# The exact half of each activation's two-part form comes from a second ReLU on ScalarE instead of a copy on VectorE

## The chip, the core and the metric

The kernel runs on one core of a Trainium2 chip. The metric is the device time of one execution, in microseconds (us). Four engines matter: TensorE (PE; its weight loads are shown apart, as PEld), VectorE (DVE), ScalarE (ACT) and the queue that issues transfers (SP). Each takes its own instructions in program order, and they meet only through semaphores.

## What is computed

The reference is the top of a recommendation model: the dot products between all pairs of 27 embeddings of a sample, and then five dense layers.

```python
bottom_mlp_output = bottom_output[:, 0, :]                     # (2048, 128)
interaction = jnp.einsum('bnd,bmd->bnm', bottom_output, bottom_output)
interaction_flat = interaction[:, _TRIL_R, _TRIL_C]            # 351 pairs
x = jnp.concatenate([bottom_mlp_output, interaction_flat, zero_pad], axis=1)
x = jax.nn.relu(x @ W0.T + b0)     # 1024
x = jax.nn.relu(x @ W1.T + b1)     # 1024
x = jax.nn.relu(x @ W2.T + b2)     # 512
x = jax.nn.relu(x @ W3.T + b3)     # 256
return x @ W4.T + b4               # 1
```

All of it is float32.

## The kernel before, in words

**Two parts for each number.** TensorE multiplies in the type `f32r`, which holds fewer bits than float32. So every operand is kept as a high part, the value rounded to `f32r`, and a low part, the value minus its high part. A product is three matmuls (`product`, L790 to L792): low weights times high activations, high times high, high times low. Three matmuls of 512 columns follow one another every 0.69 us.

**Chunks, tiles and steps.** The 2048 samples are worked in 4 chunks of 512. In a chunk, layer 0 makes 8 output tiles of 128 features by 512 samples (4 steps of one product each), layer 1 makes 8 tiles (8 steps each), and after layer 1's tile m the four products of layer 2 that use tile m-1 follow (4 steps). Layer 3 makes two tiles and layer 4 the answer. Tiles of layers 0 and 1 alternate between the two PSUM banks of `work`; layers 2 and 3 use the banks of `acc`. Of the next chunk, layer 0's tile 0 is put ahead of this chunk's layer 3, and tile 1 behind it. In the first chunk layer 0 is made in two halves of 256 samples: the left ones by functions of their own (`relu_left`, `split_left`), which the change leaves alone, and the right ones by `relu` and `split`.

**Pairs for the next chunk.** While a chunk's layers run, TensorE also makes the dot products (grams) of the next chunk's samples. At steps that `plan` lists, some three steps apart, it does a half: four matmuls into the two banks of `gps` (`gram_half`, L815). ScalarE copies each half out with four instructions (L416), and TensorE may begin the next half only when they are done (`pe.wait_ge(grams_out, n)`). VectorE prepares the inputs (L546, L548), adds the copied grams (L564), and, four times a chunk, transposes them (L605) and picks the pairs (L609); TensorE turns these (L828), ScalarE writes their high part (L440) and VectorE their low part (L627).

**What happens to a tile.** When a tile is done, ScalarE's `relu` (L442) adds the bias, applies ReLU and writes float32 into one of the two slots of `act_out` (L448). VectorE's `split` (L630) rounds that into the high part `h1h` or `h2h` (L636), and subtracts this from the value for the low part `h1l` or `h2l` (L638). Three things wait for this:
- TensorE begins the tile after next when the ReLU of the bank's last tile is done (`relu_done`);
- TensorE uses a tile as activations when its low part is there (`split_done`); layer 4 takes the high part as soon as `hi_done` says so;
- ScalarE writes a slot of `act_out` when the tile two before has been split (`split_done`).

**Orders.** All loops are unrolled in one common order (`interleave`), and every engine takes its own instructions out of that: where the order says half, then tile, ScalarE copies the half first and then applies the ReLU, whichever is ready first. In the first chunk the weights of layers 1 to 3 are also split, at the steps in `W1_AT`, `W2_AT` and `W3_AT`: ScalarE writes their high parts (L475, L464, L468), VectorE their low parts (L662, L667, L672).

Of the kernel before, what the change touches and what calls it, by code (L numbers as in the profile page):

```python
# [75 lines left out]
def rec_program(nc, x_t, x0_t, w0, w1, w2, w3, w4, biases, b4, out):  # L76
    f32, f32r = mybir.dt.float32, mybir.dt.float32r
    ALU = mybir.AluOpType
    ACT = mybir.ActivationFunctionType

    ctx = ExitStack()
    with ctx:
        def sb(name, shape, dt=f32):
            return ctx.enter_context(nc.sbuf_tensor(name, shape, dt))

        def sem(name):
            return ctx.enter_context(nc.semaphore(name))
# [17 lines left out]
        bias = sb("bias", [P, MT0 + MT1 + MT2 + MT3])  # L105
# [15 lines left out]
        h1h, h1l = sb("h1h", [P, MT0, CHUNK], f32r), sb("h1l", [P, MT0, CHUNK], f32r)  # L121
        h2h, h2l = sb("h2h", [P, 2, CHUNK], f32r), sb("h2l", [P, 2, CHUNK], f32r)
# [5 lines left out]
        H3 = MT0 - MT2  # L128

        work = ctx.enter_context(nc.psum_tensor("work", [P, 2, BANK], f32))  # L130
        acc = ctx.enter_context(nc.psum_tensor("acc", [P, 4, BANK], f32))
# [27 lines left out]
        hi_done, split_done = sem("hi_done"), sem("split_done")  # L159
        logits_done, ysum_done, y_done, out_done = sem("logits_done"), sem("ysum_done"), sem("y_done"), sem("out_done")  # L160

        def ge(eng, s, value):

            if not (isinstance(value, int) and value <= 0):
                eng.wait_ge(s, value)

        def at_first(c):

            return isinstance(c, int) and c == 0
# [27 lines left out]
        def nth(c, layer, m, more=True):  # L197

            if layer == 0 and m < EARLY:
                return m if at_first(c) else TILES * c + (m - EARLY if m == 0 else m)  # L200
            first = {0: 0, 1: MT0, 2: MT0 + MT1, 3: MT0 + MT1 + MT2 + (1 if more else 0)}
            return TILES * c + first[layer] + m

        def slot(layer, m, more=True):
            return nth(0, layer, m, more) % 2 if (layer, m) != (0, 1) else 1
# [41 lines left out]
        def columns(c):  # L247

            return RIGHT if at_first(c) else slice(0, CHUNK)
# [31 lines left out]
        def interleave(c, on_half, on_turn, on_tile, after_tile, on_step=lambda step: None):  # L281

            half_at, turn_at = plans[c]
            step = 0

            def passed(steps):
                nonlocal step
                for step in range(step, step + steps):
                    if step in half_at:
                        on_half(half_at[step])  # L290
                    if step in turn_at:
                        on_turn(turn_at[step])
                    on_step(step)
                step += 1

            for m in range(EARLY, MT0):
                passed(KT0)
                on_tile(0, m)
            for m in range(MT1):
                passed(KT1)  # L300
                on_tile(1, m)
                if m:
                    passed(MT2)
                after_tile(m)
            passed(MT2)
# [98 lines left out]
        def _(act):  # L404
            def grams_from_psum(g, h):

                n = HALVES * g + h
                act.wait_ge(gram_done, n + 1)
                if h % 2 == 0 and h >= 4:
                    act.wait_ge(half_sums, SLICES * (g - 1) + h // 2 - 1)  # L410
                at = h % 2 * HALF_GROUPS
                for q in range(GROUP):
                    rows = slice(q * QUAD, (q + 1) * QUAD)
                    src = gps[rows].rearrange("p b (g w) -> p (b g) w", w=2 * P)[:, :, 0:2 * GCOLS]
                    src = src.rearrange("p g (t c) -> p g t c", c=GCOLS)
                    last = act.activation(grams2[rows, h // 2 % 2, at:at + HALF_GROUPS, :, :],  # L416
                                          src[:, :, :, q * EVEN:q * EVEN + INPUTS], ACT.Copy)
                last.then_inc(grams_out, 1)
# [16 lines left out]
            def pairs_hi_part(g, s, first=False):  # L435

                act.wait_ge(pairs_t, SUBS * g + s + 1)
                dst = featH[0:PAIRS_TILE, 1:KT0, s * SUB:(s + 1) * SUB]
                src = pair_bank(first)[0:PAIRS_TILE, 0:PAIR_TILES * SUB].rearrange("p (t b) -> p t b", b=SUB)
                act.activation(dst, src, ACT.Copy).then_inc(pairs_hi, 1)  # L440

            def relu(c, layer, m, bank, more=True):  # L442

                n, row = nth(c, layer, m, more), [0, MT0, MT0 + MT1, MT0 + MT1 + MT2][layer] + m
                act.wait_ge(tile_done, n + 1)
                ge(act, split_done, n - 1)
                cols = columns(c) if layer == 0 else slice(0, CHUNK)
                act.activation(act_out[:, slot(layer, m, more), cols], bank[:, cols], ACT.Relu,  # L448
                               bias=bias[:, row:row + 1]).then_inc(relu_done, 1)

# [11 lines left out]
            def w2_hi_part(n):  # L462
                act.wait_ge(w2_in[n], 16)
                act.activation(w2_part(w2h, n), w2_part(w2raw, n), ACT.Copy).then_inc(w2_hi, 1)  # L464

            def w3_hi_part():
                act.wait_ge(w3_in, 16)
                act.activation(w3h[:, :], w3raw[:, :], ACT.Copy).then_inc(w3_hi, 1)  # L468

            def w1_hi_part(m):  # L470
                act.wait_ge(w_in[m % 2], kept(m))
                if m >= 2:
                    act.wait_ge(tile_done, nth(0, 1, m - 2) + 1)
                    act.wait_ge(w1_kept[m % 2], kept(m - 2))
                act.activation(w1s[:, m % 2, 0, :], stage[:, m % 2, :], ACT.Copy).then_inc(w1_hi, 1)  # L475
# [21 lines left out]
            def body(c, more):  # L497
                def on_half(h):
                    if more:
                        grams_from_psum(c + 1, h)  # L500

                def on_turn(s):
                    if more:
                        pairs_hi_part(c + 1, s)

                def on_tile(layer, m):
                    relu(c, layer, m, work[:, m % 2, :])

                def after_tile(m):
                    pass  # L510

                def on_step(step):
                    if c == 0 and step in W1_AT:
                        w1_hi_part(W1_AT[step])
                    if c == 0 and step in W2_AT:
                        w2_hi_part(W2_AT[step])
                    if c == 0 and step == W3_AT:
                        w3_hi_part()

                interleave(c, on_half, on_turn, on_tile, after_tile, on_step)  # L520
                for m in range(MT2):
                    relu(c, 2, m, acc[:, m, :])
                if more:
                    relu(c + 1, 0, 0, work[:, 0, :])
                for m in range(MT3):
                    relu(c, 3, m, acc[:, m, :], more)
                if more:
                    relu(c + 1, 0, 1, work[:, 1, :])

            for m in range(EARLY):  # L530
                relu(0, 0, m, work[:, m, :])
            for c in range(CHUNKS):
                body(c, c + 1 < CHUNKS)

# [2 lines left out]
        def _(dve):  # L537
# [92 lines left out]
            def split(c, layer, m, hi, lo, more=True):  # L630


                n, cols = nth(c, layer, m, more), columns(c) if layer == 0 else slice(0, CHUNK)
                full, hi, lo = act_out[:, slot(layer, m, more), cols], hi[:, cols], lo[:, cols]
                dve.wait_ge(relu_done, n + 1)
                dve.tensor_copy(hi, full).then_inc(hi_done, 1)  # L636
                dve.wait_ge(hi_done, n + 1)
                dve.tensor_tensor(lo, full, hi.bitcast(f32), ALU.subtract).then_inc(split_done, 1)  # L638

            def answers(c):  # L640
# [89 lines left out]
            def body(c, more):  # L730
# [8 lines left out]
                def on_tile(layer, m):  # L739
                    if layer == 0:  # L740
                        split(c, 0, m, h1h[:, m, :], h1l[:, m, :])
                        if c and m == EARLY + 1:
                            answers(c - 1)
                        if c == 0 and m == MT0 - 1:
                            w1_lo_part(1)
                    else:
                        split(c, 1, m, h2h[:, m % 2, :], h2l[:, m % 2, :])
# [14 lines left out]
                for m in range(MT2):  # L762
                    split(c, 2, m, h1h[:, H3 + m, :], h1l[:, H3 + m, :])
# [245 lines left out]
```

## Time and profile before

| what | value |
|---|---|
| time, three runs | 484.17, 484.64, 485.58 us; median 484.64 |
| profiled execution: its own time | 484.05 us |
| profiled execution: its span | 482.3 us |
| mean granted clock of TensorE | 0.996 |
| busy: PE / PEld / DVE / ACT | 470.3 / 399.2 / 282.8 / 242.6 us |

The span runs from the first instruction to the end of the last; 1.8 us of the execution's own time lie around it. A busy share is the part of the span in which the engine had at least one instruction under way. For TensorE the ends of matmuls are modelled and neighbours overlap, so its busy time doesn't tell how well it is used: the distance between starts does.

### The profile page before, as it was taken

The page shows a single profiled execution, that of the slowest core. Times are in us where ns is not written, and L with a number is a line of the kernel's source. Part 1 is how long each engine was busy: PE and PEld are TensorE (multiplying, and loading weights), DVE is VectorE, ACT ScalarE, POOL GpSimd, SP SyncE. Part 2 cuts the span into 40 slices and gives each one's busy share as a digit, 9 for nine tenths or more (in the row PEclk, how much of TensorE's full clock was granted, in tenths as well). Part 3 has the DMA queues.
Part 4 walks back from the last instruction along what each step waited for, and adds up shares of the span by engine and source line. Part 5 has one row for each costly group of instructions (what it writes and reads, how often), then busy time and mean ns, then how long its engine had stood idle before and what let it go on. Part 6 is the DMA issues. An engine that isn't in the chain of part 4 may idle for free.

```text
span 482.3 us, 6717 instructions
## 1 busy us (share of the span) xinstructions
PE 470.3 (98%) x2495; PEld 399.2 (83%) x2495; DVE 282.8 (59%) x508; ACT 242.6 (50%) x580; POOL 0.7 (0%) x6
## 2 busy tenths in 40 slices
PE   8989999999997999999999999999999999999997
PEld 8979987878775888888888888888888888888885
DVE  4599779687765877575616877766624633110124
ACT  4996577758673366565653266665553321110112
POOL 0000000000000000000000000000000000000000
PEclk9999999999998999999999999999999999999999
DMA  8979555765273231843345141653224000434200
GB/s 306 379 253 390 175 163 187 253 218 190 87 270 139 85 101 39 307 150 134 103 183 212 44 141 37 219 222 130 87 96 167 1 0 1 175 101 161 87 1 1
DMA packets 18992, 72.28 MB, mean 150 GB/s; under 512 B 2448, under 2 KB 4496, under 8 KB 14864
## 3 DMA queue, kind: packets, MB, share of 16 engines
q1 hardware_dynamic: 18960, 71.86, 42.3%
q8 instruction: 20, 0.33, 0.3%
q14 instruction: 12, 0.10, 0.1%
HBM read 63.45 MB, written 8.40 MB: 149 GB/s over the span
## 4 chain that ended last, share of the span: by engine, by line
PE 82%; DVE 9%; DMA 4%; ACT 2%; issue 2%; SPq 0%; DVEq 0%; ACTq 0%
PE work L790 18%; PE work L792 17%; PE work L791 17%; PE gps L815 8%; PE acc L790 7%; PE acc L791 6%; PE acc L792 6%; DMA xraw<-x_t 4%; DVE turned L605 2%; ACT grams L416 1%; PE acc L912 1%; DVE turned L594 1%; PE gps L828 1%; DVE w1s L662 1%; DVE pairs L609 1%
## 5 line engine op out<-in xcount | busy, mean ns | idle before, releaser
L416 ACT ACTIVATE grams<-gps 32x216 f32<-32x216 f32 x384 | 131.5, 343 | 86.0 <-PE gps L815 82.5
L790 PE MATMUL work<-h1h,w1s 128*128 128x512 f32 x256 | 101.7, 397 | 0.5 <-DVE w1s L662 0.4
L792 PE MATMUL work<-h1l,w1s 128*128 128x512 f32 x256 | 100.4, 392 | 0.0
L791 PE MATMUL work<-h1h,w1s 128*128 128x512 f32 x256 | 100.2, 391 | 0.0
L448 ACT ACTIVATE act_out<-work,bias 128x512 f32<-128x512 f32 (+1 forms) x64 | 42.3, 662 | 90.9 <-PE work L792 89.6
L815 PEld LDWEIGHTS gps<-xs 128*128 128x128 f32 x384 | 56.6, 190 | 10.0 <-issue 1.4
L636 DVE CAST h2h<-act_out 128x512 fp32r<-128x512 f32 x40 | 17.0, 426 | 76.5 <-ACT act_out L448 76.5
L815 PE MATMUL gps<-xs 128*128 128x224 f32 x384 | 58.3, 274 | 0.4 <-DVE featL L627 0.3
L790 PE MATMUL work<-featH,w0l 126*128 126x512 f32 (+5 forms) x160 | 56.7, 354 | 1.1 <-ACT act_out L448 0.6
L792 PEld LDWEIGHTS work<-h1l,w1s 128*128 128x128 f32 x256 | 48.1, 188 | 10.6
L790 PEld LDWEIGHTS work<-h1h,w1s 128*128 128x128 f32 x256 | 48.3, 189 | 9.3 <-DVE w1s L662 1.4
L792 PE MATMUL work<-featL,w0h 126*128 126x512 f32 (+5 forms) x160 | 55.7, 348 | 0.0
L791 PE MATMUL work<-featH,w0h 126*128 126x512 f32 (+5 forms) x160 | 55.7, 348 | 0.0
L564 DVE SCALAR_TENSOR_TENSOR grams<-grams 128x216 f32<-128x216 f32 x48 | 18.4, 383 | 63.1 <-ACT grams L416 62.9
L791 PEld LDWEIGHTS work<-h1h,w1s 128*128 128x128 f32 x256 | 48.4, 189 | 7.8
L790 PE MATMUL acc<-h2h,w2l 128*128 128x512 f32 x128 | 51.5, 402 | 3.0 <-DVE h2l L638 2.5
L548 DVE TENSOR_TENSOR xs<-xraw,xs 128x864 fp32r<-128x864 f32 x48 | 50.8, 1059 | 1.7
L791 PE MATMUL acc<-h2h,w2h 128*128 128x512 f32 x128 | 50.8, 397 | 0.0
L792 PE MATMUL acc<-h2l,w2h 128*128 128x512 f32 x128 | 50.8, 397 | 0.0
L636 DVE CAST h1h<-act_out 128x512 fp32r<-128x512 f32 (+1 forms) x48 | 19.3, 402 | 25.6 <-ACT act_out L448 25.4
L790 PEld LDWEIGHTS work<-featH,w0l 126*128 126x128 f32 (+2 forms) x160 | 30.1, 188 | 5.0 <-issue 1.0
L792 PEld LDWEIGHTS work<-featL,w0h 126*128 126x128 f32 (+2 forms) x160 | 30.0, 187 | 4.2
(71 smaller groups left out, 520.5 us busy)
## 6 DMA issues: line engine op xcount, KB each, us to landing
xraw<-x_t SPq DMA_DIRECT2D x64, 432.0 KB, 4.2
w1s<-w_parts SPq DMA_DIRECT2D x24, 1024.0 KB, 4.8
w_parts<-w1s SPq DMA_DIRECT2D x8, 1024.0 KB, 4.8
stage<-w_t SPq DMA_DIRECT2D x8, 512.0 KB, 5.9
w0raw<-w_t SPq DMA_DIRECT2D x4, 512.0 KB, 8.0
w2raw<-w_t SPq DMA_DIRECT2D x4, 512.0 KB, 9.0
x0raw<-x_t SPq DMA_DIRECT2D x4, 256.0 KB, 5.3
w3raw<-w_t SPq DMA_DIRECT2D x1, 512.0 KB, 10.5
```

The source lines that it names most:

```text
L416: last = act.activation(grams2[rows, h // 2 % 2, at:at + HALF_GROUPS, :, :], src[:, :, :, q * EVEN:q * EVEN + INPUTS], ACT.Copy)
L448: act.activation(act_out[:, slot(layer, m, more), cols], bank[:, cols], ACT.Relu, bias=bias[:, row:row + 1]).then_inc(relu_done, 1)
L548: dve.tensor_tensor(lo, by_sample(xraw, p), hi.bitcast(f32), ALU.subtract).then_inc(xl_done, 1)
L564: dve.scalar_tensor_tensor(out=grams[:, at:at + SLICE_GROUPS, :], in0=grams2[:, p % 2, :, 0, :], scalar=0.5, in1=grams2[:, p % 2, :, 1, :] ...
L594: dve.transpose(turned[:, :, :], first_grams(s).rearrange("p g m -> p m g")).then_inc(turned_done, 1)
L605: dve.transpose(turned[:, :, :], grams[:, :, :].rearrange("p g m -> p m g")).then_inc(turned_done, 1)
L609: dve.tensor_tensor(dst, one, other, ALU.add).then_inc(pairs_done, 1)
L636: dve.tensor_copy(hi, full).then_inc(hi_done, 1)
L790: pe.matmul(dst, wl, ah, start=start, stop=False)
L791: pe.matmul(dst, wh, ah, start=False, stop=False)
L792: return pe.matmul(dst, wh, al, start=False, stop=stop)
L815: last = pe.matmul(gps[:, j // 2, j % 2 * 2 * P:j % 2 * 2 * P + 2 * GCOLS], xs[:, p % XSLOTS, 0, four, :].rearrange("p b n -> p (b n)"), x ...
```

## The change

`relu` gets one more instruction, ahead of the old one: a ReLU of the same PSUM tile with the same bias, written as `f32r` directly to the high part. `split` loses its rounding copy and only subtracts. The semaphore `hi_done` is now raised by ScalarE. The waits ahead of `relu` now stand ahead of both its instructions. TensorE's and SP's programs stay as they are.

```diff
@@ scalar
-            def relu(c, layer, m, bank, more=True):
+            def relu(c, layer, m, bank, hi, more=True):
                 n, row = nth(c, layer, m, more), [0, MT0, MT0 + MT1, MT0 + MT1 + MT2][layer] + m
                 act.wait_ge(tile_done, n + 1)
                 ge(act, split_done, n - 1)
                 cols = columns(c) if layer == 0 else slice(0, CHUNK)
+                act.activation(hi[:, cols], bank[:, cols], ACT.Relu, bias=bias[:, row:row + 1]).then_inc(hi_done, 1)
                 act.activation(act_out[:, slot(layer, m, more), cols], bank[:, cols], ACT.Relu,
                                bias=bias[:, row:row + 1]).then_inc(relu_done, 1)
...
-                    relu(c, layer, m, work[:, m % 2, :])
+                    relu(c, layer, m, work[:, m % 2, :], h1h[:, m, :] if layer == 0 else h2h[:, m % 2, :])
...
-                    relu(c, 2, m, acc[:, m, :])
+                    relu(c, 2, m, acc[:, m, :], h1h[:, H3 + m, :])
...
@@ vector, in split
                 full, hi, lo = act_out[:, slot(layer, m, more), cols], hi[:, cols], lo[:, cols]
+                dve.wait_ge(hi_done, n + 1)
                 dve.wait_ge(relu_done, n + 1)
-                dve.tensor_copy(hi, full).then_inc(hi_done, 1)
-                dve.wait_ge(hi_done, n + 1)
                 dve.tensor_tensor(lo, full, hi.bitcast(f32), ALU.subtract).then_inc(split_done, 1)
```

The other calls of `relu` get their high part in the same way. The inserted line makes the old ReLU line L449 of the changed kernel, and its new one L448.

ScalarE, first chunk, layer 1, a place where the high part of a block of `w1` is written just ahead of a tile's ReLU. Before:

```order
L475 ACTIVATE w1s<-stage 128x1024
L448 ACTIVATE act_out<-work,bias 128x512
L416 ACTIVATE grams<-gps 32x216 x4
L464 ACTIVATE w2h<-w2raw 128x1024
L416 ACTIVATE grams<-gps 32x216 x12
```

Now:

```order
L476 ACTIVATE w1s<-stage 128x1024
L448 ACTIVATE h2h<-work,bias 128x512
L449 ACTIVATE act_out<-work,bias 128x512
L416 ACTIVATE grams<-gps 32x216 x4
L465 ACTIVATE w2h<-w2raw 128x1024
L416 ACTIVATE grams<-gps 32x216 x12
```

One instruction more stands between the block of weights and the copying of the next half.

VectorE at the end of the first chunk's layer 1: the last grams are added, transposed and picked, and then the last tile is split. Before:

```order
L564 SCALAR_TENSOR_TENSOR grams<-grams 128x216
L605 STREAM_TRANSPOSE turned<-grams 128x864
L609 TENSOR_TENSOR pairs<-turned 128x144
L609 TENSOR_TENSOR pairs<-turned 128x72
L609 TENSOR_TENSOR pairs<-turned 128x36
L609 TENSOR_TENSOR pairs<-turned 128x72
L609 TENSOR_TENSOR pairs<-turned 128x54
L636 CAST h2h<-act_out 128x512
L638 TENSOR_TENSOR h2l<-act_out,h2h 128x512
```

Now:

```order
L565 SCALAR_TENSOR_TENSOR grams<-grams 128x216
L606 STREAM_TRANSPOSE turned<-grams 128x864
L610 TENSOR_TENSOR pairs<-turned 128x144
L610 TENSOR_TENSOR pairs<-turned 128x72
L610 TENSOR_TENSOR pairs<-turned 128x36
L610 TENSOR_TENSOR pairs<-turned 128x72
L610 TENSOR_TENSOR pairs<-turned 128x54
L638 TENSOR_TENSOR h2l<-act_out,h2h 128x512
```

The rounding copy is gone; nothing else moved.

## Rows read from the trace of the kernel before

**Rows 1.** The page: busy us, share, count; share of the last chain.

```profile
PE 470.3 (98%) x2495; PEld 399.2 (83%) x2495; DVE 282.8 (59%) x508; ACT 242.6 (50%) x580; POOL 0.7 (0%) x6
...
PE 82%; DVE 9%; DMA 4%; ACT 2%; issue 2%; SPq 0%; DVEq 0%; ACTq 0%
```

**Rows 2.** Groups by form: count, busy us, mean ns, idle before.

```profile
L448 ACT ACTIVATE act_out<-work,bias 128x512 f32<-128x512 f32 x56 | 38.6, 689 | 88.9 <-PE work L792 87.7 <-DVE h1l L638 0.4
...
L638 DVE TENSOR_TENSOR h2l<-act_out,h2h 128x512 fp32r<-128x512 f32 x40 | 27.7, 692 | 1.4
...
L636 DVE CAST h2h<-act_out 128x512 fp32r<-128x512 f32 x40 | 17.0, 426 | 76.5 <-ACT act_out L448 76.5
```

**Rows 3.** Timeline, first chunk's layer 0: start us, us, instruction.

```profile
56.13 0.84 ACT L448 ACTIVATE act_out<-work,bias 128x256 f32<-128x256 f32 x2
...
56.66 0.39 PE L790 MATMUL work<-featH,w0l 128*128 128x256 f32 x1 [0.58 <-ACT act_out L448]
...
63.64 0.47 ACT L448 ACTIVATE act_out<-work,bias 128x256 f32<-128x256 f32 x1
...
64.24 0.45 PE L790 MATMUL work<-h1h,w1s 128*128 128x512 f32 x1
```

**Rows 4.** Timeline, first chunk's layer 1, weights ahead of a ReLU.

```profile
90.12 0.69 ACT L448 ACTIVATE act_out<-work,bias 128x512 f32<-128x512 f32 x1
...
90.71 1.39 ACT L416 ACTIVATE grams<-gps 32x216 f32<-32x216 f32 x4
...
92.20 0.68 PE L815 MATMUL gps<-xs 128*128 128x224 f32 x4
```

**Rows 5.** Timeline, the same pattern twice more.

```profile
102.55 0.68 PE L815 MATMUL gps<-xs 128*128 128x224 f32 x4
...
103.30 0.19 PEld L790 LDWEIGHTS work<-h1h,w1s 128*128 128x128 f32 x1 [0.25 <-DVE w1s L662]
...
133.66 1.39 ACT L416 ACTIVATE grams<-gps 32x216 f32<-32x216 f32 x4
...
135.17 0.66 PE L815 MATMUL gps<-xs 128*128 128x224 f32 x4
```

**Rows 6.** Timeline, a wait of TensorE for pairs.

```profile
81.01 0.42 DVE L636 CAST h2h<-act_out 128x512 fp32r<-128x512 f32 x1
...
83.69 0.55 DVE L627 TENSOR_TENSOR featL<-gps,featH 126x384 fp32r<-126x384 f32 x1
...
84.38 0.68 PE L815 MATMUL gps<-xs 128*128 128x224 f32 x4 [0.34 <-DVE featL L627]
```

**Rows 7.** Timeline, end of the first chunk's layer 1.

```profile
142.35 0.38 DVE L564 SCALAR_TENSOR_TENSOR grams<-grams 128x216 f32<-128x216 f32 x1 [2.45 <-ACT grams L416]
...
145.66 0.42 DVE L636 CAST h2h<-act_out 128x512 fp32r<-128x512 f32 x1
...
146.12 0.69 DVE L638 TENSOR_TENSOR h2l<-act_out,h2h 128x512 fp32r<-128x512 f32 x1
...
146.87 0.68 PE L790 MATMUL acc<-h2h,w2l 128*128 128x512 f32 x1 [2.54 <-DVE h2l L638]
```

**Rows 8.** Sums of a stretch: us, busy of PE, PEld, DVE, ACT, POOL, clock, DMA.

```profile
147.00:150.40 3.40, 3.40 (x9) 2.62 (x10) 0.00 (x0) 0.00 (x0) 0.00 (x0) 0.50 0.56 234
```

**Rows 9.** Timeline, second chunk's layer 0.

```profile
173.85 0.69 ACT L448 ACTIVATE act_out<-work,bias 128x512 f32<-128x512 f32 x1
...
174.96 1.40 ACT L416 ACTIVATE grams<-gps 32x216 f32<-32x216 f32 x4 [0.42 <-PE gps L815]
...
176.84 0.61 PE L815 MATMUL gps<-xs 128*128 128x224 f32 x4
```

**Rows 10.** Timeline, the last chunk's layers 2 and 3.

```profile
468.50 1.38 ACT L448 ACTIVATE act_out<-acc,bias 128x512 f32<-128x512 f32 x2 [2.74 <-PE acc L792]
...
472.87 0.69 DVE L638 TENSOR_TENSOR h1l<-act_out,h1h 128x512 fp32r<-128x512 f32 x1
...
473.62 0.50 PE L790 MATMUL acc<-h1h,w3l 128*128 128x512 f32 x1
```

More of the change, by code:

```diff
@@ L521, in body @@
                 for m in range(MT2):
-                    relu(c, 2, m, acc[:, m, :])
+                    relu(c, 2, m, acc[:, m, :], h1h[:, H3 + m, :])
                 if more:
-                    relu(c + 1, 0, 0, work[:, 0, :])
+                    relu(c + 1, 0, 0, work[:, 0, :], h1h[:, 0, :])
                 for m in range(MT3):
-                    relu(c, 3, m, acc[:, m, :], more)
+                    relu(c, 3, m, acc[:, m, :], h2h[:, m, :], more)
                 if more:
-                    relu(c + 1, 0, 1, work[:, 1, :])
+                    relu(c + 1, 0, 1, work[:, 1, :], h1h[:, 1, :])
             for m in range(EARLY):
-                relu(0, 0, m, work[:, m, :])
+                relu(0, 0, m, work[:, m, :], h1h[:, m, :])
             for c in range(CHUNKS):
```

## The prediction

> **What bounds the kernel now.** Start at the top of the page: TensorE is busy 98% of the span, VectorE 59% and ScalarE 50%, and 82% of the last chain is TensorE's [rows 1]. So work taken from VectorE or given to ScalarE counts only where TensorE waits for one of them. The second view is the list of TensorE's waits, read together with the timeline around each. Nearly all lie in the first chunk, where the other two engines also split the weights, and at the very end. Two kinds are to be seen. TensorE may wait for **ScalarE's queue**: for a ReLU that frees a `work` bank [rows 3], or for the copying of a half of the grams, which stands behind a ReLU [rows 4, 5]. And it may wait for **VectorE's queue**: for pairs [rows 6] or for the low part of a tile [rows 7, 10]. In chunks two and three TensorE doesn't wait: the copying ends at 174.96 + 1.40 = 176.36, and TensorE begins the next half at 176.84 [rows 9].
>
> **The prices.** A rounding copy costs VectorE 0.43 us, with the gap behind it 0.46 (145.66 to 146.12) [rows 2, 7]. A ReLU of 512 columns costs ScalarE 0.69 [rows 2]. The new ReLU has no row of its own, and the question is how much later it makes what comes behind it. The upper bound is its whole 0.69 (0.47 for 256 columns). The lower bound is what rows show of neighbours that overlap: two ReLUs of 256 columns take 0.84 together where one takes 0.47 [rows 3], so the second begins 0.10 early; and a copying begins at 90.71, 0.10 before the ReLU of 90.12 + 0.69 = 90.81 ends [rows 4]. The pair at the end that takes 1.38, twice 0.69 [rows 10], looks like the other bound, but there the second tile is finished just 0.69 behind the first (three matmuls), so its ReLU couldn't begin sooner. In the new order both ReLUs of a tile have the same waits, so nothing holds the second back. I take **0.59 for 512 columns and 0.37 for 256**.
>
> The Trainium skill ("ScalarE: Activation LUTs", section "What ACT_TABLE_LOAD costs") says the same of neighbours, "Back-to-back ACTIVATEs overlap by ≈ 93 ns", and the 0.10 above agrees. Its section "Rules for kernel authors" speaks against the change: for ReLU and the like "Use VectorE, not ScalarE". The durations here agree in direction, 0.43 on VectorE against 0.59 to 0.69 on ScalarE. By that rule alone all 88 tiles would be a loss; by the rows only those count for which TensorE waits, and the sum goes by these.
>
> **Part 1, added to ScalarE.**
> - *Start of layer 0, right half.* TensorE begins tile 4 at 56.66, 0.06 behind the first of the two ReLUs (56.13 + 0.47) [rows 3]. That ReLU is now second in its pair: **+0.37**. Layer 1's first tile begins at 64.24, 0.13 behind the ReLU of 63.64 + 0.47 [rows 3]: hardly any room, so again **+0.37**.
> - *Weights ahead of a ReLU.* Three times a block of weights and a ReLU stand between two copyings. The copying ends at 90.71 + 1.39 = 92.10 and TensorE's next half starts at 92.20, as soon as it may; the third place is the same, 133.66 + 1.39 = 135.05 against 135.17 [rows 4, 5]. Each pays the full 0.59. At the second, TensorE waits right afterwards for a block of `w1` from VectorE, until 103.30, and that wait isn't moved; 0.23 of its 0.25 us cover the delay [rows 5]. Sum: 3 x 0.59 - 0.23 = **+1.54**.
> - *Chunks two and three.* After a ReLU at 173.85 the next copying could begin at 173.85 + 2 x 0.59 = 175.03, instead of 174.96 [rows 9]: 0.07 late. Up to three such ReLUs follow each other, so 0.2 late; the copying has 0.48 - 0.10 = 0.38 to spare. **0**. With 0.69 a ReLU it would be 1.40 + 1.38 = 2.78 for a half that comes every 2.5 us (three steps of 0.69 and some 0.4 for the half itself), the spare time would be gone at the second ReLU, and each chunk would lose about 1.1.
>
> **Part 2, removed from VectorE.**
> - *Pairs.* TensorE waits 0.34 for `featL` at 84.38, which VectorE begins late, at 83.69, because it is busy without a break from before the copy of 81.01 [rows 6]. Without that copy most of the wait goes: **-0.3**.
> - *Low part of the last tile of layer 1.* TensorE waits 2.54 us, until 146.87. The chain is: grams added at 142.35, transposed, picked, copy at 145.66, subtraction at 146.12 [rows 7]. The ReLU was long done. Without the copy: **-0.46**. What is late next is the transposing, which nothing here touches.
> - The copies before 142 don't help here: VectorE had stood idle 2.45 us before 142.35, waiting for ScalarE [rows 7].
>
> **Part 3, the end.** The last chunk has no layer 0 to hide layer 3's start. Before, VectorE sets the pace with a copy and a subtraction a tile; the last subtraction begins at 472.87 and TensorE goes on at 473.62 [rows 10]. Now ScalarE sets it: eight ReLUs from 468.50 end at 468.50 + 7 x 0.59 + 0.69 = 473.32, plus 0.03, plus a subtraction of 0.69, plus 0.05 is 474.09: **+0.47**. The last tile of layer 3 then pays 0.59 - 0.46 = **+0.13**. In the other chunks layer 0's tile 0 (12 matmuls, 2.75 us) stands before layer 3 and covers this.
>
> Elsewhere a tile has 2 us or more until it is used (four products of layer 2, or most of a layer 1 tile), and the high parts that layer 4 takes come 0.4 sooner on ScalarE, but its low parts decide.
>
> **Sum.** 0.74 + 1.54 - 0.3 - 0.46 + 0.60 = **+2.1 us**: 484.05, the profiled execution's own time, becomes 486.2. The median shown is 0.59 above that execution, so I forecast **486.7** for the median. About 0.3%, 1.5 us, is what a measurement of this kernel can tell from no change.
>
> **The rivals.**
> - **A, the two ReLUs don't overlap** (0.69 each). The terms become 0.94, 3 x 0.69 - 0.2, -0.3, -0.46; chunks two and three lose 1.1 each; the first chunk's layer 3 waits 0.7, since ScalarE needs 8 x 0.69 = 5.5 us for four tiles and TensorE has 2.75 + 3 x 0.69 = 4.8 us of other work before it wants the fourth; the end takes 8 x 0.69 less what it takes now, 1.2, and 0.23. Sum 6.5: **491.2**. For it: a new destination type. Against: [rows 3, 4].
> - **B, TensorE's clock doesn't fall.** The granted clock was 0.50, 1.2 GHz, from 147.0 to 150.4, just after the wait of 2.54 us [rows 8, 7]. Half the speed over 3.4 us costs 1.7. The wait becomes 2.54 - 0.46 = 2.1 us, and if the clock stays up, the sum is 2.1 - 1.7 = +0.4, **485.0**, no change. The spread of the three runs, 1.4 us, is of this size, so this could come and go.
> - **C, VectorE's relief decides (the other side).** If VectorE's own backlog, and not ScalarE, were what makes the chain of 142.35 late, all delays of ScalarE in the first chunk would vanish in the 2.54 us wait, and seven copies of layer 1 less would end that wait: -2.5 + 0.6 = -1.9, **482.7**. It decides if VectorE no longer stands idle before L564. Against it are the 2.45 us of idle time there [rows 7].
> - **D, small delays add up elsewhere**, where the copyings have 0.38 to spare: 487.5 to 489.
>
> **How the numbers follow.** Forecast 0.50, of which 0.09 within 0.3% of before (its own range is 485.5 to 488.0); A 0.14; B 0.18, nearly all within; C 0.13; D 0.05. Slower 0.41 + 0.14 + 0.03 = 0.58, no change 0.09 + 0.18 = 0.27, faster 0.15, which takes C and the lower edge of B. The range 483.9 to 490.0 leaves out C and the upper half of A.
>
> **What the profile of the changed kernel would show.** L448 and L449 0.58 to 0.59 apart (A: 0.69). In the three places TensorE's half starts 0.6 later behind the block of weights. VectorE's last subtraction of the first chunk's layer 1 starts right behind the picking of pairs, and TensorE's wait there is 2.1 us. In chunks two and three the halves stay 2.5 us apart. The last chunk's layer 3 goes on 0.5 later. The forecast would be wrong if two of the three ScalarE places cost nothing, or if the clock behaves otherwise than before.

## The result, and the profile after

| | before | changed |
|---|---|---|
| median of 20 runs | 484.73 us | 486.37 us |
| lowest and highest | 482.92, 487.03 us | 485.03, 487.76 us |
| profiled execution: own time, span | 484.05, 482.3 us | 486.30, 484.5 us |

The changed kernel takes 1.0036 times the time of before (95% interval 1.0024 to 1.0049): 1.2 to 2.4 us slower. The medians are 1.64 us apart. The forecast was +2.1 us, to 486.7.

The page of the changed kernel, in answer to [rows 1]:

```profile
PE 470.5 (97%) x2495; PEld 399.0 (82%) x2495; DVE 248.5 (51%) x420; ACT 286.5 (59%) x668; POOL 0.7 (0%) x6
```

VectorE lost 34 us of work and ScalarE gained 44, each more than twenty times what the kernel lost. Since TensorE's program is the same, its instructions can be matched one by one. How far each begins behind its twin of before changes only in a few places; all differences in the account below were read that way.

**How two ReLUs stand to each other.** The changed kernel's timeline, ScalarE in the second chunk's layer 0, and TensorE's halves there, in answer to [rows 9]:

```profile
175.34 0.69 ACT L448 ACTIVATE h1h<-work,bias 128x512 fp32r<-128x512 f32 x1
175.93 0.68 ACT L449 ACTIVATE act_out<-work,bias 128x512 f32<-128x512 f32 x1
176.50 1.38 ACT L416 ACTIVATE grams<-gps 32x216 f32<-32x216 f32 x4
177.91 0.69 ACT L448 ACTIVATE h1h<-work,bias 128x512 fp32r<-128x512 f32 x1
178.50 0.68 ACT L449 ACTIVATE act_out<-work,bias 128x512 f32<-128x512 f32 x1
179.06 1.39 ACT L416 ACTIVATE grams<-gps 32x216 f32<-32x216 f32 x4
...
175.81 0.60 PE L815 MATMUL gps<-xs 128*128 128x224 f32 x4
178.34 0.61 PE L815 MATMUL gps<-xs 128*128 128x224 f32 x4
180.87 0.60 PE L815 MATMUL gps<-xs 128*128 128x224 f32 x4
```

A ReLU takes 0.69 but the next begins 0.57 to 0.60 behind its start (median 0.585 over 80 pairs), and the copying 0.57 behind the second one. ScalarE is now without a break here, yet TensorE's halves stay 2.53 us apart: the copying ends at 176.50 + 1.38 = 177.88, 0.46 ahead of 178.34.

**A place that pays.** The changed kernel's timeline where a block of `w1` stands ahead of the ReLUs, in answer to [rows 4]:

```profile
90.10 1.06 ACT L476 ACTIVATE w1s<-stage 128x1024 fp32r<-128x1024 f32 x1
91.19 0.69 ACT L448 ACTIVATE h2h<-work,bias 128x512 fp32r<-128x512 f32 x1
91.77 0.68 ACT L449 ACTIVATE act_out<-work,bias 128x512 f32<-128x512 f32 x1
92.34 1.38 ACT L416 ACTIVATE grams<-gps 32x216 f32<-32x216 f32 x4
...
93.82 0.34 PE L815 MATMUL gps<-xs 128*128 128x224 f32 x1 [0.60 <-issue]
```

The copying ends at 93.72 and TensorE begins at 93.82, as closely behind as before. TensorE now stands idle 0.60 ahead of that; the profile puts it down to "issue", since the semaphore it waited for has no releaser in the records, but TensorE's program waits there for the copying of the last half, and this is the only instruction that ends just ahead.

**A place that gains.** VectorE and TensorE at the end of the first chunk's layer 1, in answer to [rows 7]:

```profile
144.76 0.38 DVE L565 SCALAR_TENSOR_TENSOR grams<-grams 128x216 f32<-128x216 f32 x1 [2.44 <-ACT grams L416]
...
147.15 1.01 DVE L610 TENSOR_TENSOR pairs<-turned 128x144 f32<-128x144 f32 x5
148.07 0.69 DVE L638 TENSOR_TENSOR h2l<-act_out,h2h 128x512 fp32r<-128x512 f32 x1
...
148.81 0.50 PE L790 MATMUL acc<-h2h,w2l 128*128 128x512 f32 x1 [2.08 <-DVE h2l L638]
```

TensorE's wait is 2.08 instead of 2.54. VectorE's idle time ahead of L565 is 2.44 where it was 2.45: rival C had named that as its mark, and it didn't move.

**The end.** The last chunk's layers 2 and 3, ScalarE, then TensorE, in answer to [rows 10]:

```profile
470.10 0.69 ACT L448 ACTIVATE h1h<-acc,bias 128x512 fp32r<-128x512 f32 x1 [2.17 <-PE acc L792]
...
474.10 0.73 ACT L449 ACTIVATE act_out<-acc,bias 128x512 f32<-128x512 f32 x1
...
475.68 0.50 PE L790 MATMUL acc<-h1h,w3l 128*128 128x512 f32 x1 [0.19 <-DVE h1l L638]
...
481.55 0.61 PE L912 MATMUL acc<-w4s,h2l 128*128 128x2 f32 x4 [0.77 <-DVE h2l L638]
```

From the first ReLU to layer 3's fourth tile it is 475.68 - 470.10 = 5.58 us, where it was 473.62 - 468.50 = 5.12.

### The profile page after: what moved, and what is told of

Same layout as the page of the kernel before. It is cut to its first block, busy times and chain, and to the rows that moved or that the text cites. A ratio compares the mean times of both kernels' runs of the same rounds, so it can differ in the third digit from the quotient of the medians.

```text
span 484.5 us, 6805 instructions
## 1 busy us (share of the span) xinstructions
PE 470.5 (97%) x2495; PEld 399.0 (82%) x2495; DVE 248.5 (51%) x420; ACT 286.5 (59%) x668; POOL 0.7 (0%) x6
## 4 chain that ended last, share of the span: by engine, by line
PE 85%; DVE 5%; DMA 4%; ACT 2%; issue 2%; SPq 0%; ACTq 0%; DVEq 0%
PE work L790 18%; PE work L792 18%; PE work L791 18%; PE gps L815 9%; PE acc L790 7%; PE acc L792 7%; PE acc L791 7%; DMA xraw<-x_t 4%; DVE turned L606 1%; PE acc L912 1%; ACT grams L416 1%; PE gps L828 1%; DVE turned L595 1%; DVE xpad L682 1%; ACT act_out L449 1%
## 5 line engine op out<-in xcount | busy, mean ns | idle before, releaser
L638 DVE TENSOR_TENSOR h2l<-act_out,h2h 128x512 fp32r<-128x512 f32 x40 | 27.7, 691 | 94.6 <-ACT act_out L449 94.3
L448 ACT ACTIVATE h2h<-work,bias 128x512 fp32r<-128x512 f32 x32 | 22.0, 689 | 60.8 <-PE work L792 60.3
L638 DVE TENSOR_TENSOR h1l<-act_out,h1h 128x512 fp32r<-128x512 f32 (+1 forms) x48 | 31.1, 648 | 45.4 <-ACT act_out L449 45.4
L565 DVE SCALAR_TENSOR_TENSOR grams<-grams 128x216 f32<-128x216 f32 x48 | 18.4, 383 | 62.1 <-ACT grams L416 61.8
L449 ACT ACTIVATE act_out<-work,bias 128x512 f32<-128x512 f32 (+1 forms) x64 | 41.9, 655 | 0.0
```

Source lines behind the costliest of these rows:

```text
L448: act.activation(hi[:, cols], bank[:, cols], ACT.Relu, bias=bias[:, row:row + 1]).then_inc(hi_done, 1)
L565: dve.scalar_tensor_tensor(out=grams[:, at:at + SLICE_GROUPS, :], in0=grams2[:, p % 2, :, 0, :], scalar=0.5, in1=grams2[:, p % 2, :, 1, :] ...
```

## The experiments

All kernels were timed beside the kernel before on the same chip. Its median was 484.42 us for the first four and 485.01 for the last four; differences below are to these medians.

### The ScalarE part alone

```diff
             def relu(c, layer, m, bank, more=True):
                 ...
+                act.activation(spare[:, n % 2, cols], bank[:, cols], ACT.Relu, bias=bias[:, row:row + 1])\
+                   .then_inc(spare_done, 1)
                 act.activation(act_out[:, slot(layer, m, more), cols], bank[:, cols], ACT.Relu,
```

> The extra ReLU alone: ScalarE writes it to a spare tile that no product reads, and VectorE still makes the rounding copy. My account: the delays of part 1 stay (0.37 twice, 0.59 three times less 0.23, 0.08 at the first block of w2), nothing is given back at 84 and 146 us, and the end pays 0.93 for the four tiles and 0.59 for the last: +3.9 us, about 488.6. Rival C (VectorE's own backlog sets the long wait of the first chunk): the first chunk's delays vanish in that wait and only the end is left, +1.5, about 486.3. Rival A (no overlap of the two ReLUs): spacing 0.69 and +8 or more, with chunks two and three slower.

Measured: 491.98 us, the median of only five runs, 1.0138 times before (1.0107 to 1.017), which is 5.2 to 8.2 us more; the medians are 7.6 apart. My +3.9 was a miss. Part of the 7.6 is the clock: the run with a mean clock of 0.996 took 490.75 us, and the kernel before beside it 484.3 at the same clock, +6.4. The time speaks against rival C's +1.5. Rival A's "+8 or more" it can't rule out, but the trace below does: the two ReLUs start 0.58 apart (198.76 and 199.34), not 0.69. By the matched starts the places that I had named cost about what I had said (+0.36, +0.31, +0.56, +0.56 - 0.34, +0.55; the end +1.2 and +0.65), but there were two more. In the first chunk, the waits for layer 3's third and fourth tile cost 0.7. And four times in chunks two and three TensorE lost 0.39 at a half that follows the pairs. With what the clock did set apart, the matched starts give +6.4 in all. The timeline of this kernel at the first of the four:

```profile
198.76 0.69 ACT L449 ACTIVATE spare<-work,bias 128x512 fp32r<-128x512 f32 x1
199.21 0.49 PE L832 MATMUL gps<-ident,pairs 128*126 128x128 f32 x3
199.34 0.68 ACT L451 ACTIVATE act_out<-work,bias 128x512 f32<-128x512 f32 x1
199.91 0.49 ACT L441 ACTIVATE featH<-gps 126x384 fp32r<-126x384 f32 x1
200.13 0.43 DVE L640 CAST h2h<-act_out 128x512 fp32r<-128x512 f32 x1 [0.85 <-ACT act_out L451]
200.59 0.69 DVE L642 TENSOR_TENSOR h2l<-act_out,h2h 128x512 fp32r<-128x512 f32 x1
201.20 0.55 DVE L630 TENSOR_TENSOR featL<-gps,featH 126x384 fp32r<-126x384 f32 x1
201.90 0.68 PE L819 MATMUL gps<-xs 128*128 128x224 f32 x4
```

The low part of the pairs (L630), for which TensorE's next half waits, stands in VectorE's queue behind copy and subtraction of a tile whose ReLU is 0.6 late. In the changed kernel the same place has the late ReLU without the copy:

```profile
196.15 0.68 ACT L449 ACTIVATE act_out<-work,bias 128x512 f32<-128x512 f32 x1
...
196.93 0.69 DVE L638 TENSOR_TENSOR h2l<-act_out,h2h 128x512 fp32r<-128x512 f32 x1 [1.30 <-ACT act_out L449]
197.54 0.55 DVE L628 TENSOR_TENSOR featL<-gps,featH 126x384 fp32r<-126x384 f32 x1
198.41 0.60 PE L815 MATMUL gps<-xs 128*128 128x224 f32 x4
```

`featL` is done 0.3 ahead of TensorE's start, so TensorE isn't held up. The missing copy therefore hides here what the second ReLU would cost: my zero for chunks two and three was the sum of two terms of which I had seen none.

### The VectorE part alone

```diff
                 dve.wait_ge(relu_done, n + 1)
-                dve.tensor_copy(hi, full).then_inc(hi_done, 1)
-                dve.wait_ge(hi_done, n + 1)
                 dve.tensor_tensor(lo, full, hi.bitcast(f32), ALU.subtract).then_inc(split_done, 1)
```

> The missing copy alone: VectorE only subtracts, ScalarE makes one ReLU as before; the high parts are not written at all but cleared once at the start, so the answer leaves them out, and layer 4 waits for the low part instead of the high one. My account: -0.42 at the pairs near 84 us, -0.46 at the low part of layer 1's last tile, -1.2 at the end, where VectorE's copy no longer sets the pace, and -0.46 at the last tile: -2.5 us, about 482.2. Rival C: the seven copies of layer 1 before the long wait count too, and it all but vanishes: -4.5, about 480.2.

Measured: 482.46 us, 0.9963 (0.9945 to 0.9981), -2.0. Matched to before, TensorE gains 0.46 at the pairs, 0.47 at the low part, and 1.3 in the last chunk's layer 3 and 4 (1.2 of it up to layer 3's fourth tile). In between there is only a different course of the clock near 150 us. The last tile gave no 0.46 of its own, because this kernel's layer 4 waits for the low part only: the low part is there sooner, at 479.22 us, but TensorE then has the high part's matmuls still to do, from 479.28 to 479.74. Rival C's 2 us more are not there.

By the matched starts, clock apart, the two parts alone are +6.4 and -2.25, together +4.2, and the whole change is +1.9. The difference of 2.2 to 2.3 is just what the ScalarE part alone lost at its two further places, 0.7 and 4 x 0.39: there the missing copy takes away what the second ReLU would cost.

### The first chunk, and the later chunks

Each tile has the form of before or the new one, by a condition; `high_wait` waits for ScalarE's or VectorE's own semaphore, according to who writes the tile's high part.

```diff
+        def paired(c, layer, m):
+            return c == 0          # the other kernel: c > 0
...
+                if FLAGS[n]:
+                    act.activation(hi[:, cols], bank[:, cols], ACT.Relu, bias=bias[:, row:row + 1])\
+                       .then_inc(hi_scalar, 1)
                 act.activation(act_out[:, slot(layer, m, more), cols], bank[:, cols], ACT.Relu,
...
-                dve.tensor_copy(hi, full).then_inc(hi_done, 1)
-                dve.wait_ge(hi_done, n + 1)
+                if not FLAGS[n]:
+                    dve.tensor_copy(hi, full).then_inc(hi_done, 1)
+                high_wait(dve, n)
```

> The changed form for the tiles of the first chunk only, the form of before for the rest. My account: all of the change's delays and gains before 150 us and none at the end: +1.3 us, about 486.1. If the loss were spread over all chunks in small amounts (rival D), it would be a quarter of the whole, +0.4.

Measured: 485.34 us, 1.0018 (0.9997 to 1.0039), +0.9. The interval holds my +1.3 and also no loss at all, so the time alone decides little. The matched starts do: +0.36 and +0.34 in layer 0, +0.09 near 78 us, -0.41 at the pairs, +0.57, +0.57 - 0.33, +0.56, -0.47 at the low part, and nothing behind 152 us. Between 147 and 151 us TensorE gained 1.57 because its clock, other than in the trace of before, stayed up.

> The changed form for chunks two to four only. My account: nothing in chunks two and three, where the copying of the grams has room, and +0.6 at the end: about 485.3. Rival D (small delays add up in chunks two and three): +1 to +2.

Measured: 484.81 us, 1.0004 (0.9981 to 1.0027). The interval, -0.9 to +1.3 us, holds my +0.6, no change at all, and the lower edge of rival D's +1 to +2, so the matched starts have to decide. In them there is nothing over 0.07 between 152 and 470 us, +0.4 up to layer 3's fourth tile, and +0.1 for the last. Rival D, small delays in chunks two and three, is not there.

### The suspected cost once more

```diff
+                act.activation(spare[:, n % 2, cols], bank[:, cols], ACT.Relu, bias=bias[:, row:row + 1])\
+                   .then_inc(spare_done, 1)
                 act.activation(hi[:, cols], bank[:, cols], ACT.Relu, bias=bias[:, row:row + 1]).then_inc(hi_done, 1)
                 act.activation(act_out[:, slot(layer, m, more), cols], bank[:, cols], ACT.Relu,
```

> The suspected cost once more: a third ReLU of each tile, to a spare tile, ahead of the two. My account says that chunks two and three had about 0.4 us to spare at each copying of the grams and that one more ReLU of 0.59 used it up: now TensorE's halves in layer 0 of chunks two and three come 3.2 instead of 2.5 us apart where a tile lies between, each of these chunks loses 3 us or more, every chunk's layer 3 waits for ScalarE, and the whole is 20 us or more slower than before (505 to 510). If a ReLU simply had a price that the kernel pays wherever it stands (the changed kernel's +1.7 for 88 of them), the third would give +3.5, about 488.

Measured: 511.27 us in the single run that was made, +26 against the median of before. Its timeline, ScalarE and TensorE in the second chunk's layer 0:

```profile
182.69 0.69 ACT L449 ACTIVATE spare<-work,bias 128x512 fp32r<-128x512 f32 x1
183.28 0.68 ACT L451 ACTIVATE h1h<-work,bias 128x512 fp32r<-128x512 f32 x1
183.85 0.69 ACT L452 ACTIVATE act_out<-work,bias 128x512 f32<-128x512 f32 x1
184.42 1.38 ACT L417 ACTIVATE grams<-gps 32x216 f32<-32x216 f32 x4
...
186.10 0.60 PE L819 MATMUL gps<-xs 128*128 128x224 f32 x4
189.04 0.68 PE L819 MATMUL gps<-xs 128*128 128x224 f32 x4 [0.24 <-issue]
192.17 0.68 PE L819 MATMUL gps<-xs 128*128 128x224 f32 x4 [0.36 <-issue]
```

With three ReLUs the halves come 3.1 us apart where tiles lie between, as the 1.41 + 3 x 0.57 of ScalarE demand. Measured against the kernel before, the change with its second ReLU costs 1.6 us in all; the third ReLU adds 25. That is how near its edge the changed kernel stands in the chunks where nothing was lost.

### All but five tiles

```diff
-            return c == 0
+            return (c, layer, m) not in ((0, 0, 2), (0, 0, 6), (0, 1, 2), (0, 1, 3), (0, 1, 6))
```

> The changed form for all tiles but five of the first chunk: layer 0's tiles 2 and 6 and layer 1's tiles 2, 3 and 6, which keep the copy on VectorE. My account: the whole loss before 150 us lay in these five; left are +0.08, -0.42, -0.46 and the end's +0.6: -0.2 us, no difference that can be measured, 484.3 where before is 484.5. If the loss were a sum over many tiles, 83 of 88 changed tiles would leave most of the +1.7.

Measured: 484.81 us, 0.9987 (0.9966 to 1.0008), -0.2: no difference, as forecast. Matched to before, none of the five delays is left and both gains are (-0.41, -0.49): the loss before 150 us lay in these five tiles.

### Four chosen tiles

```diff
-            return c == 0
+            return (c, layer, m) in ((0, 1, 1), (0, 1, 7), (CHUNKS - 1, 2, 1), (CHUNKS - 1, 2, 3))
```

> The changed form where my account says that it gains, and nowhere else: layer 1's tiles 1 and 7 in the first chunk (-0.42 and -0.46), and tiles 1 and 3 of layer 2 in the last chunk, so that the two engines share the work at the end (last low part of layer 2 done 4.4 us behind the first ReLU instead of 5.1: -0.6). Sum -1.5 us, about 483.0, 0.3% faster. If the change only ever costs, it is the same or slower.

Measured: 483.81 us, 0.9975 (0.9953 to 0.9996), -1.2: faster, by little. The two gains of the first chunk are there (-0.47 each). The end gave 0.3 instead of 0.6:

```profile
469.01 0.69 ACT L469 ACTIVATE act_out<-acc,bias 128x512 f32<-128x512 f32 x1 [2.74 <-PE acc L814]
469.70 0.69 ACT L467 ACTIVATE h1h<-acc,bias 128x512 fp32r<-128x512 f32 x1
470.29 1.39 ACT L469 ACTIVATE act_out<-acc,bias 128x512 f32<-128x512 f32 x2
471.78 0.69 ACT L467 ACTIVATE h1h<-acc,bias 128x512 fp32r<-128x512 f32 x1
```

The third tile's ReLU, second of the two at 470.29, began 0.69 behind the one before it and not 0.58: it had to wait until VectorE had split the first tile, at 470.89, and so left its slot of `act_out`; it began at 470.98. I had let them overlap.

### The long wait itself

```diff
                     half_sum(g, p)
-                    if p % SLICES_SUB == SLICES_SUB - 1:
+                    if p % SLICES_SUB == SLICES_SUB - 1 and (g, p) != (1, SLICES - 1):
                         pair_products(g, p // SLICES_SUB)
...
                         split(c, 1, m, h2h[:, m % 2, :], h2l[:, m % 2, :])
+                        if c == 0 and m == MT1 - 1:
+                            pair_products(1, SUBS - 1)
```

> The kernel of the run before it, and the wait of 2.5 us taken away: in the first chunk VectorE splits layer 1's last tile ahead of the last transposing and picking of pairs instead of behind them. TensorE then waits at most 0.5 for the tile and 0.9 for the pairs three products later. I expect TensorE to begin the second chunk's layer 0 3.2 us earlier than before where the clock fell behind the long wait, 1.7 earlier where it did not, and the fall near 150 us to be gone from all runs: about -3.5 us against before, 481. If the wait only moved to the pairs, it would be as the kernel of the run before it.

Measured: 482.08 us, the median of seven runs, 0.9936 (0.991 to 0.9962), -2.9: the fastest kernel of the study, and 1.7 faster than the kernel of four chosen tiles. I had expected -3.5, 481. The timeline, VectorE and TensorE:

```profile
143.49 0.69 DVE L660 TENSOR_TENSOR h2l<-act_out,h2h 128x512 fp32r<-128x512 f32 x1 [0.91 <-ACT act_out L469]
144.10 1.93 DVE L626 STREAM_TRANSPOSE turned<-grams 128x864 f32<-128x864 f32 x1
146.06 1.02 DVE L630 TENSOR_TENSOR pairs<-turned 128x144 f32<-128x144 f32 x5
...
144.24 0.51 PE L814 MATMUL acc<-h2h,w2l 128*128 128x512 f32 x1
...
147.14 0.55 PE L852 MATMUL gps<-ident,pairs 128*126 128x128 f32 x3 [0.55 <-DVE pairs L630]
```

The tile hardly makes TensorE wait any more, the pairs make it wait 0.55, and TensorE begins the second chunk's layer 0 some 3.4 us earlier than its twin of before. Of these, 1.57 are what the fallen clock cost before. That the clock stays up near 150 us is seen in this one trace. Five of the seven runs had a mean clock of 0.995 or 0.996, about what one fall gives, so a fall was left in them; where it lay no trace shows.

## Why the prediction was right, step by step

| step | forecast us | measured us |
|---|---|---|
| layer 0, tile 4 waits for a ReLU | +0.37 | +0.35 |
| layer 1's first tile waits for a ReLU | +0.37 | +0.33 |
| block of `w2` behind ScalarE, near 78 us | not seen | +0.08 |
| weights ahead of a ReLU, three places | +1.54 | +0.55, +0.56 - 0.33, +0.55 = +1.33 |
| pairs, near 84 us | -0.3 | -0.42 |
| low part of layer 1's last tile | -0.46 | -0.46 |
| chunks two and three | 0 | +0.08 |
| end, layer 3's fourth tile | +0.47 | +0.46 |
| last tile of layer 3 | +0.13 | +0.18 |
| sum | +2.1 | +1.93 |

The measured column is read from the two profiled executions, by the matched starts of TensorE's instructions. These executions are 2.25 us apart. Of that, 0.69 arose by 28 us, where both kernels have the same instructions: a turning of pairs began at 28.17 instead of 27.48. In the other direction, the half-clock stretch and the wait for pairs behind it cost 0.43 less in the changed kernel: its lag is 1.95 at the first matmul behind the low part and 1.52 when the second chunk's layer 0 begins. What is left, 2.25 - 0.69 + 0.43 = 1.99, is the sum of the table but for 0.06 of small drifts.

The agreement of 486.37 with 486.7 is in part luck, since a median also depends on how often the clock falls. Runs of like clock agree with the account too. The changed kernel's 15 runs at 0.995 or 0.996 had a median of 486.6, its three at 0.999 one of 485.25; the kernel before, in its runs beside the experiments, had 484.4 and 483.55. That is +2.2 and +1.7. The clocks of the 20 runs of before in the result's table are not on record, so how much of its 1.64 is clock stays open.

- **The price of the second ReLU**, 0.59, was the main choice. Measured: 0.585. Rival A fell. The two rows that showed an overlap of neighbours had decided rightly, and the pair that took twice 0.69 was indeed paced by its tiles. The Trainium skill ("ScalarE: Activation LUTs", section "What ACT_TABLE_LOAD costs") gives 93 ns for the overlap; the trace agrees, with 0.69 - 0.585 = 0.10.
- **Part 1 and part 2** were right in place and size. The largest miss is the second of the three places, 0.23 instead of 0.36: the wait for `w1` gave back 0.23 as forecast, and 0.10 came on top, since before the second matmul behind that wait began 0.34 behind the first (103.30 to 103.64), and in the changed kernel, with hardly a wait left, 0.24 (105.25 to 105.49).
- **Part 3** was right, 0.46 and 0.18 where it said 0.47 and 0.13.
- **Zero in chunks two and three** was right as a number and wrong in its working. I had looked at the copying of the grams alone. The ScalarE part alone showed a second path, over the low part of the pairs in VectorE's queue, which would have cost 0.39 four times, and which the missing copy shortens by 0.46. The zero came out because these two cancel, which was luck.
- **Rival B** was right in part. The clock falls in some executions and not in others, but not because the wait got shorter (below). Where it didn't fall, 1.57 us came back, not 1.7, and the three runs of the changed kernel at 0.999 took 485.25, near the rival's 485.0; but the kernel before has such runs as well.
- **Rival C** fell: its mark didn't move, and the VectorE part alone gained 2.0, not 4.5.
- **Rival D** fell: the later chunks alone show nothing over 0.07 between 152 and 470 us.
- **Two slips in the working** change nothing: rival A's terms sum to 6.4 and not 6.5, and the chances for "slower" take 0.03 for D, which had 0.05.

## What to carry to other kernels

Moving work from one busy engine to another is worth only what the waits of the bounding engine say, place by place: here 88 tiles were changed, the cost and the gain of the first chunk lay in seven of them, and changing four chosen tiles turned the loss into a small gain. A cost that idle room hides shows in full once the room is used up: the change with the second ReLU cost 1.6 us, the third ReLU 25. When a move gives and takes at once, run each half alone: two terms that cancel look like a place where nothing happens, and the largest gain, moving the pairs behind the split, was found by asking what stood ahead of the last link of the chain.

## What the runs showed of the hardware

TensorE's clock does not follow from the length of the wait alone. Nine profiled executions have a wait of 2.05 to 2.54 us at the end of the first chunk's layer 1, all nine with the same matmuls behind it. In six the granted clock then fell to 0.50, 1.2 GHz, for 3.4 us: behind 2.54 us (before), 2.08 (changed), 2.07 (the VectorE part alone), 2.05 (all but five), 2.08 (four chosen) and 2.07 (three ReLUs). In three it stayed at 2.4 GHz: behind 2.52 (later chunks), 2.07 (first chunk) and 2.53 (the ScalarE part alone). Sums of a stretch that holds these matmuls, first for the first chunk's kernel, then for the later chunks' (columns as in [rows 8]):

```profile
147.00:151.00 4.00, 2.40 (x12) 1.98 (x13) 1.54 (x6) 0.00 (x0) 0.00 (x0) 1.00 0.94 393
```

```profile
147.00:151.00 4.00, 3.37 (x15) 2.46 (x15) 0.69 (x3) 1.14 (x3) 0.00 (x0) 1.00 0.47 199
```

There is a second such place, which has nothing to do with the change. Near 28 us TensorE waits for pairs, 1.34 to 2.43 us in the ten profiled executions. In four of them (the VectorE part alone, all but five, four chosen, the ScalarE part alone) the clock fell to 0.50 there, for 3.4 us in the first three and 6.8 in the last. In the first three that cost 0.7 us, by the matched starts. So a difference of two profiled executions holds such a part as well, and it has to be taken out before a change is priced.

Both places make one kernel's runs differ. The runs of before beside the last four kernels had a median of 483.5 us at a mean clock of 0.999 or 1.0, 484.3 at 0.995 and 485.8 at 0.992. With the long wait gone, none of seven runs had a mean clock under 0.995, against 12 of 24 for the kernel before. That fits with one of two places being gone, but seven runs are few.
